# Where the low parts of a dense chunk's weighted one-hots are written: VectorE, or ScalarE beside the high parts

## The reference

```python
h = relu(layernorm(x))
msg = h[dst] @ W_i + h[src] @ W_j + edge_attr @ W_e
msg = edge_weight[:, None] * msg
x = x + segment_sum(msg, dst, 6250) + h @ W_self
```

## Time and profile before

| | us |
|---|---|
| median of 3 runs | 1631.67 |
| lowest and highest | 1626.91, 1635.6 |
| the profiled execution, its own time | 1629.45 |
| its span in the trace | 1627.6 |

### The profile page before, as it was taken

The page is one execution under the profiler, slowest core; times in us unless marked ns, Lnnn a source line. Parts: engine busy times, 40 slices in busy tenths (PEclk is TensorE's granted clock), DMA queues, the critical chain, the costliest instruction groups (busy, mean ns, idle before and its releaser), DMA issues.

```text
span 1627.6 us, 25952 instructions
## 1 busy us (share of the span) xinstructions
PE 1400.3 (86%) x8448; PEld 1001.9 (62%) x8449; DVE 980.0 (60%) x4423; ACT 600.8 (37%) x1479; POOL 726.9 (45%) x783
## 2 busy tenths in 40 slices
PE   2587787798888887988879996999999979999996
PEld 0366566666666665656656666666666646666664
DVE  7799999998898997979889769100101030010204
ACT  5355665555656555455564336100000010020203
POOL 8777777777676776667666748000000000000000
PEclk9699999899999998989989999999999989999999
DMA  7478777899989898899889983778686838777773
GB/s 259 157 224 275 245 264 256 278 300 303 329 266 310 283 286 289 274 304 285 293 283 328 309 287 156 277 268 331 231 328 233 327 140 318 268 297 276 288 286 132
DMA packets 178853, 441.26 MB, mean 271 GB/s; under 512 B 24619, under 2 KB 104924, under 8 KB 175388
## 3 DMA queue, kind: packets, MB, share of 16 engines
q1 hardware_dynamic: 155996, 391.75, 67.0%
q0 software_dynamic: 22432, 46.97, 11.0%
q10 hardware_dynamic: 288, 0.85, 0.2%
HBM read 318.94 MB, written 120.55 MB: 270 GB/s over the span
## 4 chain that ended last, share of the span: by engine, by line
PE 62%; DVE 15%; DMA 9%; ACT 8%; POOL 2%; issue 2%; SPq 1%; DVEq 0%; ACTq 0%; POOLq 0%
PE psAE L1120 33%; PE psAE L1030 13%; DMA home<-h_table 8%; PE psAE L1062 6%; DVE home L1420 5%; ACT home L789 5%; DVE home L1424 4%; PE psW L931 3%; DVE home L1478 3%; PE psW L1049 2%; PE psW L1039 2%; ACT home L821 1%; PE psNS L1039 1%; ACT home L832 1%; POOL home L630 1%
## 5 line engine op out<-in xcount | busy, mean ns | idle before, releaser
L630 POOL DMA_INDIRECT home<-h_table,src_i x676 | 654.0, 967 | 257.8 <-issue 200.5
L1120 PE MATMUL psAE<-home 128*128 128x350 f16 x3528 | 539.3, 313 | 5.7 <-DVE home L1522 3.7
L1120 PEld LDWEIGHTS psAE<-home 128*128 128x128 f16 x3528 | 338.0, 96 | 201.8 <-issue 3.7
L1030 PE MATMUL psAE<-home 128*128 128x256 f32 x1352 | 324.3, 399 | 33.4 <-DVE home L1454 19.8
L1030 PEld LDWEIGHTS psAE<-home 128*128 128x128 f32 x1352 | 269.2, 201 | 86.0 <-issue 41.1
L1478 DVE TENSOR_SCALAR home<-iota_h,dst_rel,home 128x128 f32<-128x128 f16 x832 | 221.6, 363 | 17.9 <-PE psAE L1030 15.6
L1420 DVE TENSOR_SCALAR home<-iota_h,tile 128x245 f16<-128x245 f16 x1004 | 209.6, 302 | 27.5 <-PE psW L1049 18.6
L789 ACT ACTIVATE home<-psW 128x490 f16<-128x490 f32 x406 | 206.1, 578 | 49.8 <-PE psW L1039 40.3
L1424 DVE TENSOR_SCALAR home<-iota_h,tile 128x128 f16<-128x128 f16 x1004 | 179.4, 281 | 0.0
L1582 DVE SCALAR_TENSOR_TENSOR home<-psAE,home 128x350 f32<-128x350 f32 x18 | 9.4, 523 | 242.9 <-PE psAE L1120 238.1
L1582 DVE SCALAR_TENSOR_TENSOR home<-psAE,unscale,home 128x350 f32<-128x350 f32 x18 | 10.5, 582 | 239.5 <-PE psAE L1120 239.5
(11 more groups left out here) (211 smaller groups left out, 1220.3 us busy)
## 6 DMA issues: line engine op xcount, KB each, us to landing
home<-counts SPq DMA_DIRECT2D x36, 4287.5 KB, 13.5
counts<-home SPq DMA_DIRECT2D x126, 612.5 KB
home<-edges SPq DMA_DIRECT2D x64, 845.0 KB
weighted<-home SPq DMA_DIRECT2D x24, 1225.0 KB, 7.1
home<-weighted SPq DMA_DIRECT2D x36, 800.0 KB
home<-h_table,src_i POOLq DMA_INDIRECT x676
home<-h_table SPq DMA_DIRECT2D x36, 256.0 KB
home<-inv_row SPq DMA_DIRECT2D x36, 175.0 KB, 13.1
```

The lines of the kernel that those rows point to most:

```text
L630: pool.indirect_dma_start(out=rows[to][:, j, :], out_offset=None, in_=from_table[:, :], in_offset=bass.IndirectOffsetOnAxis(ap=src_i[b][:, ...
L1030: done = nc.tensor.matmul(psA[:, 0:2 * P].rearrange("p (n f) -> p n f", n=2), onehot[:, j, :], both_of(s, b, j), start=(j == 0), stop=(j = ...
L1120: last = nc.tensor.matmul((psA, psE)[r][:, 0:SNODES].rearrange("p (c d) -> p c d", c=SUPER), halves[:, a, n, :], tiles[:, :, a, :], start= ...
```

## The change

In `weigh_hots` ScalarE makes, for pairs 2, 3 and 4, the low one-hot of a group right behind its high one: eight activations instead of four, the second with the low part of the weight as its scale. `low_hots` is called for pairs 0 and 1 alone, so its two calls for pairs 2, 3 and for pair 4 are gone from VectorE. TensorE waits for the semaphore of the low parts only at W0 and W1, and the counts in the waits are made to fit. The same numbers are computed from the same tiles, into the same buffers.

```diff
@@ weigh_hots (ScalarE)
                 for j in range(4):
                     t, at = divmod(c * GROUPS + 4 * k + j, P)
-                    done = nc.scalar.activation(whot_all[k % 2][:, j, 0, :], ghot(4 * k + j)[1], ACT.Copy, scale=w_parts[t][:, 0, at:at + 1])
+                    for n in range(1 if k < 2 else 2):
+                        done = nc.scalar.activation(whot_all[k % 2][:, j, n, :], ghot(4 * k + j)[1], ACT.Copy, scale=w_parts[t][:, n, at:at + 1])
                 done.then_inc(whot_ready, 1)
@@ weigh_pair (TensorE)
                 pe.wait_ge(whot_ready, ORDER[i] * 5 + k + 1)
-                pe.wait_ge(whot_low, ORDER[i] * 5 + k + 1)
+                if k < 2:
+                    pe.wait_ge(whot_low, ORDER[i] * 2 + k + 1)
@@ count_groups (VectorE)
                     if half == 0:
                         node_weights(i, c)
-                        if i and ORDER[i - 1] < DENSE:
-                            low_hots(i - 1, (4,))
@@ low_hots (VectorE)
                 for k in ks:
-                    if c * 5 + k >= 2:
-                        dve.wait_ge(made, slot_end(i, "W", k - 2) if k >= 2 else slot_end(WHEN[c - 1], "W", k + 3))
+                    if c:
+                        dve.wait_ge(made, slot_end(WHEN[c - 1], "W", 4 - k))
@@ the loop over the chunks (VectorE)
                 add_sums(i, c, base)
-                if c < DENSE:
-                    low_hots(i, (2, 3))
```

## The result

| | before | changed |
|---|---|---|
| median, us | 1633.63 (4 runs) | 1651.32 (4 runs) |
| lowest and highest | 1626.91, 1636.66 | 1650.33, 1656.34 |
| the profiled execution, its own time and its span | 1629.45, 1627.6 | 1650.33, 1648.5 |

The ratio is 1.0105, with a 95% interval of 1.0078 to 1.0132: the changed kernel is some 17 us slower.

The account below looks back on a forecast made before the run. In dense cycles ScalarE's work before W4 was taken as the bound, with VectorE waiting. 14.0 us for pair 4 plus 0.1 for pairs 2 and 3 gave 14.1 us, 1646 us against the median; range 1637 to 1657 us.

Parts of the forecast that it names:

- Which view to trust: Stage of the chunks: busy shares (VectorE 89%, ScalarE 54%) against what ended last around a dense chunk; the latter was followed.
- the chain: Dense cycle: W2, ScalarE's copy of W2, its pair 4 one-hots, W4, VectorE's second half; cost 1.17 us per cycle, 14.0 us.
- The rival of relief: Whole loop: VectorE bounds the stage, so 34.7 us less work there gives 1597.0 us; chance 0.05.
- VectorE, value 0 on the path: Dense cycles: 144 one-hots, 34.7 us, leave VectorE, but it then waits longer for W4; gain 0.
- ScalarE, pair 4: 1.17 us x 12: Behind the copy of W2: eight activations instead of four delay W4 by 1.17 us in 12 cycles, 14.0 us.
- the removal of that wait: TensorE at W2, W3 and W4: the wait for VectorE's low parts was never the last one; value 0.
- Pairs 2 and 3 hidden: ScalarE ahead of the sums' copy: 2.34 us added fit 2.38 idle; 0 to 0.3 us together, 0.1 taken.
- The clock: Rival: added idle time lowers TensorE's clock, pieces in five turns lose 1.8 us each, 9 us, 1654.8 us; chance 0.12.
- the five turns that I had named: Turns 22, 26, 31, 45 and 50, with a piece between C4 and the next line 1030; 1.8 us each if slowed.
- The sum: Whole kernel: 14.0 us for pair 4 plus 0.1 for pairs 2 and 3, 14.1 us.
- the forecast itself: Whole kernel 10 to 20 us slower, likeliest 1646 us, 1641 to 1651 with the runs' noise; chance 0.72.
- Absorbed: Rival: waits for a piece's rows pay back the delay from turn 21 on, leaving 4.7 us, 1636.4 us; chance 0.11, including other small costs.

Follow-up runs that it names:

- e10: Kernel before, with the low parts of pairs 2, 3 and 4 made by no engine and ScalarE as before, repeated with 12 runs: 1.0004.
- e11: Changed kernel with ScalarE's eight one-hots of pair 4 ahead of the copy of W2 instead of behind it: 1639.29 us, 1.0031 against the kernel before.
- e3: Kernel before, with the low parts of pairs 2, 3 and 4 made by no engine and ScalarE as before, 5 runs: 0.9953.
- e1: Kernel before, with only the low parts of pairs 2 and 3 moved to ScalarE, those of pair 4 left on VectorE: 1.0009.
- e7: Repeat, against the kernel before: low parts of pairs 2 and 3 on ScalarE, those of pair 4 on VectorE: 1.0018.
- e5: The changed kernel again, unaltered, measured against the kernel before: 1653.37 us, 1.0084.

## Why the prediction was right, and where not

**Which view to trust.** Right. The busy shares (VectorE 89%) pointed to a gain, the chain and the waits of line 1049 to a loss. The rival of relief asked for 1597 us; e10 without the low parts ran at 1.0004, in a session of the long kind, and e11, with the relief, at 1.0031 in one of the usual kind. The median came to 1651.32 us, against 1646 forecast and a range of 1637 to 1657.

**VectorE, value 0 on the path.** Right. I had its wait for W4 at 7.5 to 8 us and some 92 us in all; the second half's 12 waits are 92.3 us. The 8.68 at the chunk shown holds 0.8 us of the slow W4. The row's 121.5 us in 19 waits has 29.2 us more, in 7 waits of the first half: in cycles with a late W1 it now waits where the low ones of pair 2 and 3 had waited before. Not shown in isolation is that the relief is worth exactly nothing: e3 gained some 10 us of 2035. That the turn ahead keeps its length held in sum (172.3 and 174.1 us) and not turn by turn: turn 21 grew by 4.2 us, turn 39 shrank by 2.0.

**ScalarE, pair 4: 1.17 us x 12.** Right, and slightly small. W2 to W4 grew from 3.34 to 4.55 us, 1.21 each, 14.5 us in all. Four more activations took 1.16 us from start to start (2.33 against 1.17). The other 0.04 to 0.05 us lie between the last one-hot and W4, 0.14 us instead of 0.10. They do not come from the added work, since e3 and e10 have them without it; they go with the wait for the low parts, which the change took away from W4, and why is not shown. I had called the removal of that wait worth 0. ScalarE's one-hot line has 41.7 us more busy time (117.8 - 76.1), not the 46 that I had by the mean of before.

**Pairs 2 and 3 hidden.** Right. At the chunk shown 0.42 us of idle time are left of 2.38; in 9 of the 12 cycles none is left, and in turn 36 the copy comes some 0.5 us late, as forecast, and in turn 54 too. W2 to W4 is 4.56 us in those two turns against 4.55, so at most 0.01 us reached W4, and e1 and e7 show W2 to W4 at 3.34 to 3.36. I had allowed 0 to 0.3 us for them; e7's interval does not exclude more, in its other kind of session.

**The clock.** I gave it 0.12, as a rival beside the forecast, of 9 us in five turns. It was no alternative but an addition: behind the dense turns every trace of the changed kernel lost 4.1 to 6.5 us more than the chain explains, and my sum had no term for it. That is the term that was mis-sized, 0 instead of about 5. In the profile of the changed kernel 1.6 us of the 6.5 are W4's in turns 13 and 17, which I had not named. Nearly all of the rest is in the five turns that I had named: 26 lost nothing, and 22, 31, 45 and 50 lost 1.1 to 1.4 us each beyond the 1.21. There the rows show the clock as well. C2 and C3, C4 and the piece in turn 22, and the granted clock over C2 to C4 (columns of the earlier trace rows), first before, then in the changed kernel:

```profile
383.36 1.00 PE L1039 MATMUL psW<-home 128*128 128x245 f16 x8 [2.38 <-DVE home L1424]
384.20 0.58 PE L1039 MATMUL psNS<-home 128*128 128x245 f16 x4
384.62 2.85 PE L1062 MATMUL psAE<-home 128*128 128x400 f32 x8
383.30:384.70 1.40, 1.34 (x13) 1.28 (x14) 1.36 (x6) 0.72 (x2) 1.09 (x2) 1.00 1.00 420
```

```profile
394.93 1.80 PE L1040 MATMUL psW<-home 128*128 128x245 f16 x8 [2.29 <-DVE home L1426]
396.52 1.02 PE L1040 MATMUL psNS<-home 128*128 128x245 f16 x4
397.35 3.29 PE L1064 MATMUL psAE<-home 128*128 128x400 f32 x8
394.90:397.40 2.50, 2.47 (x13) 1.89 (x14) 2.46 (x11) 1.46 (x4) 1.89 (x3) 0.50 0.93 299
```

From C2's start to the piece's it took 2.42 us instead of 1.26, and from there to the next line 1030 3.13 instead of 2.84. C2 to C4 stood at 0.50 in all four turns that lost time and at 1.00 in turn 26. So the rival had the turns right and the place wrong: in turns 22 and 31 most of the loss is in C2 to C4, ahead of the piece, which it had not priced. Its 1.8 us (5.70 - 3.91) also took for full speed a piece that ran at a granted clock of 0.73; the pieces of turns 22, 26 and 31 had taken about 2.9 us. That the widened gap brings the fall is shown for W4 (14 of 48 cycles against none of 120). For C2 to C4 it is not: in e5, the same kernel, these five turns lost 1.8 us beyond the chain and not 5.1, and e11, with a gap 0.29 us wider than before, lost 1.7 in them. The Trainium skill, TensorE: Matmul & The Clock Gate, HAM oscillation, warns of such idle gaps; the trace agrees for W4 of turns 13 and 17, where the clock fell inside the gap that the change had widened (0.97 to 0.50), while in most of the other cycles, behind as long a gap, W4 ran at full speed. That filling the gap saves time in the whole kernel, I could not show.

**The sum.** 14.1 forecast, 20.9 us between the spans and 17 us by the ratio. The two measures differ since the profiled execution of the kernel before lay 4.2 us under its median and that of the changed one 1.0. Chain 14.5 and the rest of 6.5 make the 21.0 of the table; that the other differences (+1.8, -4.5, -0.2, +2.7) nearly cancel was not forecast. The other turns are 2.7 to 6.4 us shorter in all five later traces of the usual kind than in the one of before; whether part of the delay is paid back there is not shown. The chain, forecast to 0.4 us, kept the median inside the range; 1651.32 is just above the 1641 to 1651 that I had given the forecast itself, by the clock's part.

**Absorbed.** It fell: TensorE's waits for the pieces did not shrink in the changed kernel. The row of it that answers to the earlier trace rows (here up to 1010 us):

```profile
PE psAE L1064 <- DMA home<-h_table: 23.8, 13, 3.3
```

It was 18.8 us. So nothing was paid back in these waits, and the two spans differ by 20.9 us, as much as was lost behind the dense turns. Why these waits grew by 5 us stays open.

## What to carry to other kernels

An engine that is busy 89% of a stage need not be what the stage waits for at the place where its work is taken; look at what ended the wait of the instruction behind it. Work moved to an idle engine costs by its place in that engine's queue: eight activations instead of four put 14.5 us on the chain where they stood behind a copy, and 3.5 where they stood ahead of it. Before moving work, see whether something that nobody waits for stands ahead of it in the queue, and exchange the two first.

## What the runs showed of the hardware that I had not expected

The same kernel took 1632 to 1637 us in three sessions and 2010 to 2035 us in three, with either kind on each of two chips, and with the difference in waits that the trace calls remote (315.3 us in 25 waits at one line of ScalarE) and in single instructions about a microsecond apart, while the local distances were the same to 0.02 us: W2 to W4 was 3.34 us in the kernel before and 3.34 to 3.36 in e1 and e7, which leave pair 4 alone. With the wait for VectorE's low parts gone from W4, W4 started 0.14 us behind ScalarE's last one-hot instead of 0.10, in all 12 cycles of each trace (e3 and e10 against e1 and e7). TensorE's clock, kept at 2.4 GHz through W4 by 20 matmuls that nobody needs, stood at 1.2 GHz 5.6 us later, behind an idle time of 2.33 us.
